# Graph layers with residual norms on one core: row sums on ScalarE, other start addresses of the operands, another order in the beginning

## The chip, the cores and the metric

The program runs on one core of a Trainium2 chip, in one launch. The metric is the device time in microseconds (us). TensorE (PE in the rows) multiplies, and loads its stationary operand by a separate instruction (PEld). VectorE is DVE, ScalarE is ACT, GpSimd is POOL, and SyncE (SP) issues nearly all DMA transfers.

## The reference, cut to what matters

For each of 16 graphs, x is 512x256 and adj is 512x512, all float32:

```python
num_neighbours = adj.sum(axis=-1, keepdims=True)
h = x @ W0 + b0
x1 = layernorm(x + (adj @ h) / num_neighbours)
x2 = relu(adj @ (x1 @ W1) + b1)
x3 = relu(adj @ (x2 @ W2) + b2)
out = layernorm(x1 + adj @ (x3 @ W3) + b3)
```

## The kernel before, in words

**Numbers.** Every matmul operand is split into a high part in the engine's rounded float32 type and a low part, the rest. ScalarE writes the high part (`copy_hi`, line 396), VectorE (`sub_hi`, line 555) or GpSimd (lines 748, 755) the low part. A product is three matmuls, high by high, high by low and low by high (`three_passes`, lines 157 to 159), so a graph takes 228 matmuls.

**Tiles.** There are T = 4 tiles of 128 nodes. A graph goes through eight products. P0 is x W0 (24 matmuls, 256 columns). P1 is adj h (48 matmuls, 258 columns: two columns of ones beside h give the row sums of adj in the same PSUM bank). P2 is the transposed adj x1 (24, 512 columns), P3 the product with W1 (12, 512), P4 with W2 (24, 256), P5 the transposed adj product of s2 (24, 512), P6 with W3 (24, 256), and P7 adj s3 (48, 256). P1 and P7 have adj as the stationary operand and h or s3 as the moving one. In P5, P2, P0, P4 and P6 s2, x1, xT, x2 and x3 are stationary and adj or the weights move. In P3 W1 is stationary and g moves.

**Order.** The order of the instructions of each engine is written out by hand, and semaphores tie the engines together. In the steady state one step (`step`, a loop over three of them) works on three graphs at once: old, new and nxt, in the order P5(old), P2(new), P6(old), P3(new), P7(old), P0(nxt), P4(new), P1(nxt). ScalarE's step follows the same order; between P7 and P1 it takes the four square roots of the second layer norm (`norm2`, line 479), each when VectorE has the moments of a tile, and then the four high parts of h (`h`). P1 waits for all four parts of h. The first two graphs have code of their own ahead of the loop, and the last ones behind it; the three P1, P7 or P5 pieces in them are the same products in smaller pieces.

**Row sums.** After P1, VectorE's `norm1` takes the reciprocal of column 256 of each of the four banks (line 590) and uses it in line 597.

**Start addresses.** On-chip tensors lie behind one another in the order of their declaration, each from the next multiple of 32 bytes. Of every partition's row, by the sizes in the code, these begin at the following remainders modulo 128:

| tensor | before | after |
|---|---|---|
| w, adj | 0 | 0 |
| xT | 0 | 64 |
| s2 | 64 | 0 |
| x1, g, x2, x3, s3 | 64 | 64 |
| h_hi / h_lo, with the bytes from tile to tile | 0 / 32, 1032 | 64 / 64, 1152 |

High and low part have the same remainder but in h before. Slices inside the tensors other than h are whole multiples of 128 bytes apart.

**The beginning.** ScalarE's queue issues the loads of W0 and of the second half of xT, SyncE's all others. A warm-up of 16 matmuls on zeros runs first. P0 of the first graph waits for the whole split of W0. SyncE loads adj of the second graph into the buffer of the first one, and so waits until the first is split (lines 180 to 183).

Of the kernel before, what the change touches and what calls it, by code (L numbers as in the profile page):

```python
# [5 lines left out]
ALU = mybir.AluOpType  # L6
# [4 lines left out]
P = 128  # L11
# [4 lines left out]
WARM = 16  # L16


def build(nc, xT, x, adjT, w0, w1, w2, w3, b0, b1, b2, b3, out):
# [8 lines left out]
    with ExitStack() as ctx:  # L28
# [9 lines left out]
        adj_raw = sb("adj_raw", [P, T, N], F32)  # L38
        w_raw = sb("w_raw", [P, 4, KF, F], F32)
# [28 lines left out]
        inv_rows = sb("inv_rows", [P, T], F32)  # L68
# [4 lines left out]
        std1 = sb("std1", [P, T], F32)  # L73
# [14 lines left out]
        adj_loaded = [sem(f"adj_half{n}_loaded") for n in range(2)]  # L88
        stored = sem("stored")
# [11 lines left out]
        adj0_last_split = sem("adj0_last_split")  # L101
# [58 lines left out]

        block = ctx.enter_context(nc.Block())

        @block.sync
        def _(sp):
# [5 lines left out]
            first_half, second_half = half_of(0, T), half_of(1, T)  # L170
            sp.dma_start(xT_raw[:, first_half], xT[0, :, first_half]).then_inc(xT0_loaded[0], DMA)
            sp.dma_start(adj_raw[:, first_half, :], adjT[0, :, first_half, :]).then_inc(adj_loaded[0], DMA)
            sp.dma_start(adj_raw[:, second_half, :], adjT[0, :, second_half, :]).then_inc(adj_loaded[1], DMA)
# [19 lines left out]
            def load(i):  # L193
# [8 lines left out]
                sp.dma_start(x_raw[:, :, :], x[i]).then_inc(x_loaded, DMA)  # L202

# [14 lines left out]
        def _(pe):  # L218
# [28 lines left out]

            def p1_first(tiles):

                for k in range(T):  # L250
                    pe.wait_ge(h_split, max(k + 1, len(tiles)))
                    if k < T - 1:
                        pe.wait_ge(adj_split, k + 1)
                    else:
                        pe.wait_ge(adj0_last_split, 1)
                    for j in tiles:
                        cols = slice(j * P, (j + 1) * P)
                        mm = three_passes(pe, bank_b[j][:, 0:F + ONES],
                                          (adj_hi[:, 0, k, cols], adj_lo[:, 0, k, cols]),
                                          (h_hi[:, k, :], h_lo[:, k, :]), k == 0, k == T - 1)  # L260
# [14 lines left out]
            def p1(new, tiles=range(T)):  # L275
# [3 lines left out]
                s = slot(new)  # L279
                for j in tiles:  # L280
# [77 lines left out]
            pe.wait_ge(w0_split, 1)  # L358
            p0(FIRST, None, None)
# [34 lines left out]
        def _(act):  # L394
# [81 lines left out]
            def norm2(old, tiles=range(T)):  # L476
                for j in tiles:
                    act.wait_ge(moments2_ready, at(old, T, j + 1))
                    act.activation(std2[:, j:j + 1], moments2[:, j, 1:2], ACT.Sqrt,  # L479
                                   bias=eps_col[:, :]).then_inc(std2_ready, 1)  # L480

            def step(new, last=False, ahead=True):
# [11 lines left out]
                if not last:  # L494
                    norm2(old)
# [27 lines left out]
            norm1(FIRST, None, range(2, T + 1))  # L523
            split_w(1)
            norm1(second, None, range(0, 1))
# [27 lines left out]
        def _(dve):  # L553
# [266 lines left out]
```

## Time and profile before

| | us |
|---|---|
| median of 3 runs | 559.99 (559.52 to 560.68) |
| the profiled execution, time of the run | 559.2 |
| its span, first to last instruction | 557.3 |
| TensorE busy | 545.2, 98% of the span |
| VectorE, ScalarE, GpSimd busy | 352.3, 275.1, 207.3 |

The span leaves 1.9 us of the run's time around it. TensorE's busy time counts overlapping matmuls once, so what a matmul costs is read from the distance of two starts, not from its own duration.

### The profile page before, as it was taken

Reading aid. Unit: us, or ns where it says so; the run is one execution under the profiler, and the core shown is the slowest. Engines: PE = TensorE matmul, PEld = TensorE weight load, DVE = VectorE, ACT = ScalarE, POOL = GpSimd, SP = SyncE. Lnnn points to the kernel's source line nnn. Section 1 sums busy time; section 2 is a strip of 40 time slices with the busy share of each in tenths; the row PEclk is TensorE's granted clock in tenths of the full one; section 3 lists DMA queues with packets and bytes.
Section 4 is the critical chain, followed back from the end, with each engine's and each line's share of the span. In section 5 each row is a group of like instructions: output and inputs, shape, how many; then the busy total and the mean of one; then the engine's idle time right before and its main releaser. Section 6 shows DMA issues by size and latency. Waiting matters only on the chain.

```text
span 557.3 us, 10510 instructions
## 1 busy us (share of the span) xinstructions
PE 545.2 (98%) x3664; PEld 499.7 (90%) x3664; DVE 352.3 (63%) x1075; ACT 275.1 (49%) x645; POOL 207.3 (37%) x224
## 2 busy tenths in 40 slices
PE   8899999999999999999999999999999999999996
PEld 8788989989899898989989899898989989899885
DVE  5764665747567475665747667475665756657455
ACT  5465454463644536454464644636454364543632
POOL 2647226081450906317071350905318072361000
PEclk9999999999999999999999999999999999999999
DMA  6900230503105050140503205040140502200002
GB/s 229 307 13 1 57 135 1 188 2 110 80 0 188 0 180 9 48 140 0 188 0 99 89 0 188 0 169 19 38 151 0 188 1 71 119 1 39 2 1 76
DMA packets 13270, 43.55 MB, mean 78 GB/s; under 512 B 1728, under 2 KB 2496, under 8 KB 13248
## 3 DMA queue, kind: packets, MB, share of 16 engines
q1 hardware_dynamic: 12960, 42.74, 22.4%
q10 hardware_dynamic: 288, 0.52, 0.3%
q8 instruction: 13, 0.21, 0.2%
q14 instruction: 9, 0.07, 0.0%
HBM read 34.87 MB, written 8.39 MB: 78 GB/s over the span
## 4 chain that ended last, share of the span: by engine, by line
PE 94%; issue 2%; DVE 2%; ACT 1%; DMA 1%; POOL 0%; POOLq 0%; DVEq 0%; SPq 0%
PE bank_a L157 16%; PE bank_a L159 16%; PE bank_a L158 16%; PE bank_b L157 15%; PE bank_b L158 15%; PE bank_b L159 15%; DMA adj_raw<-in_adjT 1%; DVE x_lo L555 0%; DVE x L604 0%; DVE v L597 0%; DVE h_lo L555 0%; POOL adj_lo L748 0%; ACT x_hi L459 0%; ACT adj_hi L396 0%; ACT bank_a L461 0%
## 5 line engine op out<-in xcount | busy, mean ns | idle before, releaser
L748 POOL TENSOR_TENSOR adj_lo<-adj_raw,adj_hi 128x512 fp32r<-128x512 f32 x61 | 77.0, 1295 | 288.3 <-ACT adj_hi L396 288.3
L555 DVE TENSOR_TENSOR x_lo<-bank_a,x_hi 128x512 fp32r<-128x512 f32 x64 | 44.3, 692 | 68.7 <-ACT bank_a L461 68.7
L157 PE MATMUL bank_b<-h_hi,adj_hi 128*128 128x258 f32 x256 | 72.4, 283 | 2.2 <-DVE h_lo L555 2.2
L158 PE MATMUL bank_b<-h_lo,adj_hi 128*128 128x258 f32 x256 | 72.3, 282 | 0.0
L159 PE MATMUL bank_b<-h_hi,adj_lo 128*128 128x258 f32 x256 | 72.2, 282 | 0.0
L157 PE MATMUL bank_b<-s_hi,adj_hi 128*128 128x256 f32 x256 | 70.9, 277 | 0.9 <-DVE s_lo L555 0.9
L159 PE MATMUL bank_b<-s_hi,adj_lo 128*128 128x256 f32 x256 | 70.7, 276 | 0.0
L158 PE MATMUL bank_b<-s_lo,adj_hi 128*128 128x256 f32 x256 | 70.7, 276 | 0.0
L436 ACT ACTIVATE std<-moments,eps_col 128x1 f32<-128x1 f32 x64 | 18.9, 295 | 93.3 <-DVE moments L616 93.3
L479 ACT ACTIVATE std<-moments,eps_col 128x1 f32<-128x1 f32 x64 | 18.9, 295 | 80.1 <-DVE moments L656 80.1
L459 ACT ACTIVATE x_hi<-bank_a,b_col 128x512 fp32r<-128x512 f32 x64 | 43.8, 684 | 21.9 <-PE bank_a L159 20.7
L736 POOL TENSOR_TENSOR x1b<-x,b_all 128x256 f32<-128x256 f32 x64 | 46.0, 757 | 18.2 <-DVE x L604 18.2
L555 DVE TENSOR_TENSOR g_lo<-bank_a,g_hi 128x512 fp32r<-128x512 f32 x32 | 22.1, 692 | 47.2 <-ACT g_hi L396 47.2
L157 PE MATMUL bank_a<-adj_hi,x_hi 128*128 128x512 f32 x128 | 50.6, 396 | 0.6 <-DVE x_lo L555 0.6
L157 PEld LDWEIGHTS bank_b<-h_hi,adj_hi 128*128 128x128 f32 x256 | 48.4, 189 | 2.4 <-DVE h_lo L555 2.3
L157 PE MATMUL bank_a<-adj_hi,s_hi 128*128 128x512 f32 x128 | 50.5, 394 | 0.0
L158 PE MATMUL bank_a<-adj_lo,x_hi 128*128 128x512 f32 x128 | 50.5, 394 | 0.0
L159 PE MATMUL bank_a<-adj_hi,x_lo 128*128 128x512 f32 x128 | 50.4, 394 | 0.0
L159 PE MATMUL bank_a<-adj_hi,s_lo 128*128 128x512 f32 x128 | 50.4, 394 | 0.0
L158 PE MATMUL bank_a<-adj_lo,s_hi 128*128 128x512 f32 x128 | 50.4, 394 | 0.0
L157 PEld LDWEIGHTS bank_b<-s_hi,adj_hi 128*128 128x128 f32 x256 | 48.0, 188 | 1.8 <-DVE s_lo L555 1.1
L158 PEld LDWEIGHTS bank_b<-s_lo,adj_hi 128*128 128x128 f32 x256 | 48.0, 188 | 0.7
(84 smaller groups left out, 1586.4 us busy)
## 6 DMA issues: line engine op xcount, KB each, us to landing
adj_raw<-in_adjT SPq DMA_DIRECT2D x32, 512.0 KB, 5.4
x_raw<-in_x SPq DMA_DIRECT2D x16, 512.0 KB, 7.4
xT_raw<-in_xT SPq DMA_DIRECT2D x15, 512.0 KB, 6.6
out_y<-y SPq DMA_DIRECT2D x15, 512.0 KB, 2.9
w_raw<-in_w SPq DMA_DIRECT2D x3, 256.0 KB, 4.3
out_y<-y SPq DMA_DIRECT2D x4, 128.0 KB, 1.9
w_raw<-in_w ACTq DMA_DIRECT2D x1, 256.0 KB, 3.5
xT_raw<-in_xT SPq DMA_DIRECT2D x1, 256.0 KB, 3.7
```

The lines of the kernel that those rows point to most:

```text
L157: pe.matmul(acc, st[0], mv[0], start=start, stop=False)
L158: pe.matmul(acc, st[0], mv[1], start=False, stop=False)
L159: return pe.matmul(acc, st[1], mv[0], start=False, stop=stop)
L436: act.activation(std1[:, j:j + 1], moments1[:, j, 1:2], ACT.Sqrt, bias=eps_col[:, :]).then_inc(std1_ready, 1)
L459: act.activation(hi[:, f, :], bank_a[f][:, :], ACT.Relu, bias=bias[:, f:f + 1])
L479: act.activation(std2[:, j:j + 1], moments2[:, j, 1:2], ACT.Sqrt, bias=eps_col[:, :]).then_inc(std2_ready, 1)
L555: return dve.tensor_tensor(lo, full, hi.bitcast(F32), ALU.subtract)
L736: pool.tensor_tensor(x1b[:, slot(batch), j, :], x1[:, j, :], b3_all[:, :], ALU.add).then_inc(x1b_ready, 1)
L748: pool.tensor_tensor(adj_lo[:, s, k, :], adj_raw[:, k, :], adj_hi[:, s, k, :].bitcast(F32), ALU.subtract).then_inc(done, 1)
```

## The change

ScalarE sums the rows of adj: SyncE loads adj, untransposed, into a new buffer (1 MB for each graph from the third on), and a copy with an accumulated output on ScalarE gives the sum of a tile's rows, one behind each square root of `norm2`. From the third graph on P1 has 256 columns, and VectorE takes one reciprocal of all four sums. The first two graphs keep the ones. The tensors are declared in another order, with the remainders of the table above, and h's tiles are 288 elements apart. In the beginning SyncE issues W0 and both halves of xT first, P0 starts on the high parts alone, h comes ahead of the adj splits, and the second graph's adj goes into the new buffer without the wait. Two more warm-up matmuls run.

```diff
-WARM = 16
+H_ROW = 288
+WARM = 18
...
         w_hi, w_lo = pair("w", [P, 4, KF, F])
+        adj_hi, adj_lo = pair("adj", [P, RING, T, N])
+        s2_hi, s2_lo = pair("s2", [P, T, F])
+        inv_rows = sb("inv_rows", [P, T], F32)
+        std1 = sb("std1", [P, T], F32)
+        x1_hi, x1_lo = pair("x1", [P, T, F])
         xT_hi, xT_lo = pair("xT", [P, T, KF, P])
-        adj_hi, adj_lo = pair("adj", [P, RING, T, N])
-        h_hi, h_lo = pair("h", [P, T, F + ONES])
-        x1_hi, x1_lo = pair("x1", [P, T, F])
         g_hi, g_lo = pair("g", [P, KF, N])
         x2_hi, x2_lo = pair("x2", [P, KF, N])
-        s2_hi, s2_lo = pair("s2", [P, T, F])
         x3_hi, x3_lo = pair("x3", [P, KF, N])
         s3_hi, s3_lo = pair("s3", [P, T, F])
+        h_hi, h_lo = pair("h", [P, T, H_ROW])
...
             sp.wait_ge(xT_split, 2)
             sp.dma_start(xT_raw[:, :], xT[1]).then_inc(xT_loaded, DMA)
-            sp.wait_ge(adj_split, T)
-            sp.wait_ge(adj0_last_split, 1)
-            sp.dma_start(adj_raw[:, first_half, :], adjT[1, :, first_half, :]).then_inc(adj_loaded[0], DMA)
-            sp.dma_start(adj_raw[:, second_half, :], adjT[1, :, second_half, :]).then_inc(adj_loaded[1], DMA)
+            for half, tiles in enumerate(halves):
+                sp.dma_start(adj1_raw[:, tiles, :], adjT[1, :, tiles, :]).then_inc(adj1_loaded[half], DMA)
...
                 sp.wait_ge(xb_ready, i * T)
                 sp.dma_start(x_raw[:, :, :], x[i]).then_inc(x_loaded, DMA)
+                sp.wait_ge(rows_ready, i * T)
+                sp.dma_start(adj_rows[:, :, :], adj[i]).then_inc(rows_loaded, DMA)
...
+            def p0_first():
+                for j in range(T):
+                    half = j // (T // 2)
+                    pe.wait_ge(xT_hi_ready, half + 1)
+                    for k in range(KF):
+                        pe.matmul(bank_b[j][:, 0:F], xT_hi[:, j, k, :], w_hi[:, 0, k, :], start=k == 0, stop=False)
+                    pe.wait_ge(w0_split, 1)
+                    for k in range(KF):
+                        pe.matmul(bank_b[j][:, 0:F], xT_hi[:, j, k, :], w_lo[:, 0, k, :], start=False, stop=False)
+                    pe.wait_ge(xT_split, half + 1)
+                    for k in range(KF):
+                        mm = pe.matmul(bank_b[j][:, 0:F], xT_lo[:, j, k, :], w_hi[:, 0, k, :],
+                                       start=False, stop=k == KF - 1)
+                    mm.then_inc(p0_done, 1)
...
+                width = F + ONES if new is second else F
...
+            def row_sum(nxt, j):
+                if j == 0:
+                    act.wait_ge(rows_loaded, at(nxt, DMA, -DMA))
+                act.activation(adj_rows[:, j, :], adj_rows[:, j, :], ACT.Copy,
+                               accum_out=rows[:, j:j + 1]).then_inc(rows_ready, 1)
...
                     act.activation(std2[:, j:j + 1], moments2[:, j, 1:2], ACT.Sqrt,
                                    bias=eps_col[:, :]).then_inc(std2_ready, 1)
+                    if nxt is not None:
+                        row_sum(nxt, j)
...
+                    if a == 0 and not from_columns:
+                        dve.wait_ge(rows_ready, at(new, T, T))
+                        dve.reciprocal(inv_rows[:, :], rows[:, :]).then_inc(inv_rows_ready, 1)
```

How the instructions move on ScalarE, in the step between the last Relu ahead of P7 and the high parts of h; before:

```order
L461 ACTIVATE bank_a<-bank_a,b_col 128x512
L479 ACTIVATE std<-moments,eps_col 128x1 x4
L421 REGISTER_ALU
L396 ACTIVATE h_hi<-bank_b 128x256
L421 REGISTER_ALU
L396 ACTIVATE h_hi<-bank_b 128x256
```

and after, at the same place:

```order
L502 ACTIVATE bank_a<-bank_a,b_col 128x512
L521 ACTIVATE std<-moments,eps_col 128x1
L456 REGISTER_ALU
L457 ACTIVATE adj_rows,rows<-adj_rows 128x512
L521 ACTIVATE std<-moments,eps_col 128x1
L457 ACTIVATE adj_rows,rows<-adj_rows 128x512
L521 ACTIVATE std<-moments,eps_col 128x1
L457 ACTIVATE adj_rows,rows<-adj_rows 128x512
L521 ACTIVATE std<-moments,eps_col 128x1
L457 ACTIVATE adj_rows,rows<-adj_rows 128x512
L462 REGISTER_ALU
L424 ACTIVATE h_hi<-bank_b 128x256
```

Four copies of 512 columns now stand between the square roots and ahead of h's high parts.

SyncE's queue from the program's start; before:

```order
L171 DMA xT_raw<-in_xT 128x512
L172 DMA adj_raw<-in_adjT 128x1024
L173 DMA adj_raw<-in_adjT 128x1024
L174 DMA x_raw<-in_x 128x1024
L175 DMA b_all<-in_b 128x256
L178 DMA xT_raw<-in_xT 128x1024
L182 DMA adj_raw<-in_adjT 128x1024
L183 DMA adj_raw<-in_adjT 128x1024
```

and after:

```order
L184 DMA w_raw<-in_w 128x512
L186 DMA xT_raw<-in_xT 128x512 x2
L188 DMA adj_raw<-in_adjT 128x1024 x2
L189 DMA x_raw<-in_x 128x1024
L190 DMA b_all<-in_b 128x256
L193 DMA xT_raw<-in_xT 128x1024
L195 DMA adj_rows<-in_adjT 128x1024 x2
```

W0 and the second half of xT came from ScalarE's queue before; now one queue has all, and the second graph's adj follows the second xT without a wait between them.

## Rows read from the trace of the kernel before

**Rows 1.** The page, busy time of each engine

```profile
PE 545.2 (98%) x3664; PEld 499.7 (90%) x3664; DVE 352.3 (63%) x1075; ACT 275.1 (49%) x645; POOL 207.3 (37%) x224
```

**Rows 2.** The page, the chain that ended last, by engine

```profile
PE 94%; issue 2%; DVE 2%; ACT 1%; DMA 1%; POOL 0%; POOLq 0%; DVEq 0%; SPq 0%
```

**Rows 3.** Timeline of TensorE, each product's first matmul; start, duration in us

```profile
175.53 0.40 PE L157 MATMUL bank_a<-adj_hi,s_hi 128*128 128x512 f32 x1
...
181.14 0.39 PE L157 MATMUL bank_a<-adj_hi,x_hi 128*128 128x512 f32 x1
...
186.74 0.28 PE L157 MATMUL bank_b<-w_hi,x_hi 128*128 128x256 f32 x1
...
189.47 0.39 PE L157 MATMUL bank_a<-g_hi,w_hi 128*128 128x512 f32 x1
...
192.22 0.28 PE L157 MATMUL bank_b<-s_hi,adj_hi 128*128 128x256 f32 x1
...
197.66 0.28 PE L157 MATMUL bank_b<-w_hi,xT_hi 128*128 128x256 f32 x1
...
200.53 0.28 PE L157 MATMUL bank_a<-w_hi,x_hi 128*128 128x256 f32 x1
...
203.36 0.28 PE L157 MATMUL bank_b<-h_hi,adj_hi 128*128 128x258 f32 x1
...
209.12 0.40 PE L157 MATMUL bank_a<-adj_hi,s_hi 128*128 128x512 f32 x1
```

**Rows 4.** The same of the last graphs: P7's first half, P4, P7's third tile, P5

```profile
528.08 0.28 PE L157 MATMUL bank_b<-s_hi,adj_hi 128*128 128x256 f32 x1
...
530.80 0.28 PE L157 MATMUL bank_a<-w_hi,x_hi 128*128 128x256 f32 x1
...
533.63 0.28 PE L157 MATMUL bank_b<-s_hi,adj_hi 128*128 128x256 f32 x1
...
535.05 0.39 PE L157 MATMUL bank_a<-adj_hi,s_hi 128*128 128x512 f32 x1
```

**Rows 5.** The same of the beginning, up to the first step's P5

```profile
1.20 3.78 PE L246 MATMUL bank_a<-zeros 128*128 128x256 f32 x16 [1.20 <-DVE zeros L673]
6.21 0.55 PE L157 MATMUL bank_b<-w_hi,xT_hi 128*128 128x256 f32 x1 [1.24 <-DVE xT_lo L555]
...
10.99 0.28 PE L157 MATMUL bank_b<-h_hi,adj_hi 128*128 128x258 f32 x1
...
16.73 0.28 PE L157 MATMUL bank_a<-w_hi,xT_hi 128*128 128x256 f32 x1
...
21.91 0.36 PE L157 MATMUL bank_b<-h_hi,adj_hi 128*128 128x258 f32 x1 [2.15 <-DVE h_lo L555]
...
41.19 0.40 PE L157 MATMUL bank_a<-adj_hi,s_hi 128*128 128x512 f32 x1
```

**Rows 6.** Timeline of the other engines in the beginning

```profile
4.31 0.43 DVE L681 CAST w_hi<-w_raw 128x512 fp32r<-128x512 f32 x1 [3.02 <-DMA w_raw<-in_w]
4.55 0.63 ACT L396 ACTIVATE xT_hi<-xT_raw 128x512 fp32r<-128x512 f32 x1 [1.39 <-DMA xT_raw<-in_xT]
...
15.95 1.15 ACT L396 ACTIVATE adj_hi<-adj_raw 128x512 fp32r<-128x512 f32 x2 [3.33 <-DMA adj_raw<-in_adjT]
...
19.32 2.49 POOL L748 TENSOR_TENSOR adj_lo<-adj_raw,adj_hi 128x512 fp32r<-128x512 f32 x2
...
19.76 1.42 DVE L555 TENSOR_TENSOR h_lo<-bank_a,h_hi 128x256 fp32r<-128x256 f32 x4 [0.94 <-ACT h_hi L396]
```

**Rows 7.** Groups by form; busy us, mean ns | idle before

```profile
L396 ACT ACTIVATE adj_hi<-adj_raw 128x512 fp32r<-128x512 f32 x64 | 39.1, 617 | 3.6 <-DMA adj_raw<-in_adjT 3.6
```

**Rows 8.** Timeline of ScalarE and VectorE, from norm2's first square root to h

```profile
195.49 0.29 ACT L479 ACTIVATE std<-moments,eps_col 128x1 f32<-128x1 f32 x1 [1.84 <-DVE moments L656]
...
199.46 0.64 ACT L396 ACTIVATE h_hi<-bank_b 128x256 fp32r<-128x256 f32 x2
...
200.12 1.46 DVE L555 TENSOR_TENSOR h_lo<-bank_b,h_hi 128x256 fp32r<-128x256 f32 x4
```

More of the change, by code:

```diff
@@ L67, in build @@
         y = sb("y", [P, T, F], F32)
-        inv_rows = sb("inv_rows", [P, T], F32)
+        rows = sb("rows", [P, T], F32)
         stats1 = sb("stats1", [P, T, 6], F32)
@@ L88, in build @@
         adj_loaded = [sem(f"adj_half{n}_loaded") for n in range(2)]
+        adj1_loaded = [sem(f"adj1_half{n}_loaded") for n in range(2)]
+        rows_loaded = sem("rows_loaded")
+        rows_ready = sem("rows_ready")
+        inv_rows_ready = sem("inv_rows_ready")
         stored = sem("stored")
@@ L168, in half_of @@
                 return slice(half * n // 2, (half + 1) * n // 2)
[L170 to L173, printed above, removed]
+            sp.sem_inc(rows_ready, 2 * T)
+            halves = [half_of(half, T) for half in range(2)]
+            sp.dma_start(w_raw[:, 0, :, :], w0).then_inc(w_loaded[0], DMA)
+            for half, tiles in enumerate(halves):
+                sp.dma_start(xT_raw[:, tiles], xT[0, :, tiles]).then_inc(xT0_loaded[half], DMA)
+            for half, tiles in enumerate(halves):
+                sp.dma_start(adj_raw[:, tiles, :], adjT[0, :, tiles, :]).then_inc(adj_loaded[half], DMA)
             sp.dma_start(x_raw[:, :, :], x[0]).then_inc(x_loaded, DMA)
@@ L178, in _ @@
             sp.dma_start(xT_raw[:, :], xT[1]).then_inc(xT_loaded, DMA)
-            sp.wait_ge(adj_split, T)
-            sp.wait_ge(adj0_last_split, 1)
-            sp.dma_start(adj_raw[:, first_half, :], adjT[1, :, first_half, :]).then_inc(adj_loaded[0], DMA)
-            sp.dma_start(adj_raw[:, second_half, :], adjT[1, :, second_half, :]).then_inc(adj_loaded[1], DMA)
+            for half, tiles in enumerate(halves):
+                sp.dma_start(adj1_raw[:, tiles, :], adjT[1, :, tiles, :]).then_inc(adj1_loaded[half], DMA)
             sp.dma_start(w_raw[:, 1, :, :], w1).then_inc(w_loaded[1], DMA)
@@ L474, in x3, with norm2 @@
                 relu_split(p5_done, old, f, b2_col, x3_hi, x3_hi_ready)
-            def norm2(old, tiles=range(T)):
+            def norm2(old, tiles=range(T), nxt=None):
                 for j in tiles:
@@ L507, in _ @@
             split_xT(FIRST, 1)
+            h(FIRST, tiles=range(0, 2))
             split_adj(FIRST, 0)
             split_adj(FIRST, 1)
-            h(FIRST, tiles=range(0, 2))
+            h(FIRST, tiles=range(2, T))
             split_adj(FIRST, 2)
             split_adj(FIRST, 3)
-            h(FIRST, tiles=range(2, T))
             split_xT(second, 0)
@@ L522, in _ @@
             h(second, bank_a)
[L523 removed]
+            norm1(FIRST, None, range(2, 3))
             split_w(1)
+            norm1(FIRST, None, range(3, T + 1))
             norm1(second, None, range(0, 1))
@@ L685, in _ @@
             split_xT(FIRST, 1)
+            h(FIRST, tiles=range(0, 2))
             split_adj(FIRST, 0)
-            h(FIRST, tiles=range(0, 1))
             split_adj(FIRST, 1)
-            h(FIRST, tiles=range(1, 2))
+            h(FIRST, tiles=range(2, T))
             split_adj(FIRST, 2)
-            h(FIRST, tiles=range(2, T))
+            split_adj(FIRST, 3)
             split_xT(second, 0)
@@ L742, in split_w, with split_adj @@
                                    ALU.subtract).then_inc(w_split, 1)
-            def split_adj(nxt, done, tiles=range(T)):
+            def split_adj(nxt):
                 s = slot(nxt)
-                for k in tiles:
+                raw = adj1_raw if nxt is second else adj_raw
+                for k in range(T):
                     pool.wait_ge(adj_hi_ready, at(nxt, T, k + 1))
-                    pool.tensor_tensor(adj_lo[:, s, k, :], adj_raw[:, k, :], adj_hi[:, s, k, :].bitcast(F32),
-                                       ALU.subtract).then_inc(done, 1)
+                    pool.tensor_tensor(adj_lo[:, s, k, :], raw[:, k, :], adj_hi[:, s, k, :].bitcast(F32),
+                                       ALU.subtract).then_inc(adj_split, 1)
             def split_xT(nxt):
@@ L771, in _ @@
             pool.wait_ge(adj_split, T)
-            split_adj(second, adj_split)
+            split_adj(second)
             add_b0(second)
@@ L803 @@
         "adjT": adj.reshape(NB, P, T, P, T).transpose(0, 3, 4, 2, 1).reshape(NB, P, T, N),
+        "adj": adj.reshape(NB, P, T, N),
     }
```

53 lines of the change are left out of this document (28 added, 25 removed).

## The prediction, as put on record before the changed kernel ran

> **What bounds the kernel now.** First the page: TensorE is busy 545.2 of 557.3 us [rows 1], and the chain that ended last is 94% TensorE [rows 2]. A faster ScalarE or VectorE is worth nothing by itself; what counts is how far apart TensorE's matmuls start, and where it waits. So I read its timeline. One step is 33.59 us [rows 3], the distance of two P5, and no start in that list has an idle time in front of it. The distances of the nine starts, divided by the matmuls in between, give what one matmul costs in each product:
>
> - P5 5.61 us / 24 = 234 ns, P2 5.60 / 24 = 233 ns, P3 2.75 / 12 = 229 ns, all with 512 columns.
> - P6 2.73 / 24 = 114 ns, P7 5.44 / 48 = 113 ns, P4 2.83 / 24 = 118 ns, P0 2.87 / 24 = 120 ns, with 256 columns, and P1 5.76 / 48 = 120 ns with 258.
>
> The same columns cost 113 ns in one product and 120 in another. Set beside the table of start addresses, the dear one of the 256-column products is P0, the only one whose stationary and moving operand both begin at remainder 0; P6, P7 and P4 have 64 on one side and 0 on the other. P1 mixes many remainders, since its tiles are 1032 bytes apart. The two extra columns of P1 explain 2/256 of 113 ns, 0.9 ns, and not 6.7.
>
> P4 shows a second thing: it has P6's remainders and costs 4.5 ns more. The end of the program helps. There P7's first half starts at 528.08 and takes 2.72 us / 24 = 113 ns, P4 directly behind it 2.83 / 24 = 118 ns, and P7's third tile behind that 1.42 / 12 = 118 ns, though it is the same product as the one at 113 [rows 4]. So a pace once taken is handed on by unbroken matmuls of 256 columns, and the passage from P7 (moving operand at 64) to a product with its stationary operand at 64 costs the fast pace.
>
> **The beginning** is 41.19 us to the first P5 [rows 5]. P0 starts at 6.21, after 1.24 us of waiting for a low part of xT, and its 24 matmuls take 4.78 us, against 2.87 later. TensorE also waits 2.15 us ahead of 21.91.
>
> The terms are taken against the profiled execution: span 557.3 us, time 559.2, which is 0.8 us below the median of the runs, 559.99. I carry the differences over to the median.
>
> **The change, part by part.**
>
> *P1, width and start of h.* 14 graphs (the third to the last) run with 256 columns and h at 64 against adj at 0, which is what P7 has. Bounds: 113 ns, P7's pace [rows 3], and 120, no gain. P1 follows P4, and P4 follows P0. In the tail the same passage, P4 to P7's third tile, stays at 118 [rows 4], so I take 117.9: 14 x 48 x 2.1 ns = 1.4 us. Lower bound 0, upper 14 x 48 x 6.7 ns = 4.5 us.
>
> *P0, xT at 64.* It now has P4's and P6's remainders. It follows P7, exactly the passage that gives 118 in the tail. 14 x 24 x (119.6 - 117.9) ns = 0.6 us; upper bound with P6's 113.8, 2.0 us. P4 behind it stays at 117.9; with the fast pace it would give 14 x 24 x 4.1 ns = 1.4 us.
>
> *P5, s2 at 0.* Now both operands begin at 0, at 512 columns. No row shows that pair at this width. The nearest rows: with 64 stationary and 0 moving 233.3 ns, with 0 and 64 229 (P3), so the start addresses do matter at 512 too. The step between paces at 256 columns is 6.7 ns (113.3 to 120.0). [...] I bound the effect at 6.7 ns per matmul to either side and take the gain, 16 x 24 x 6.7 ns = 2.6 us, as P3 shows that 233 is not the floor. This is the weakest term. P2 keeps its remainders and its 233 ns.
>
> [...]
>
> *Row sums.* Four ScalarE copies of 512 columns per step with an accumulated output. No row has that form. Bounds: 0.62 us, the plain copy [rows 7], and that plus a square root's 0.29 [rows 8], 0.91. I take 0.75. What hides them: the first square root starts at 195.49, h's first high part at 199.46, the last low part ends at 200.12 + 1.46 = 201.58, and P1 starts at 203.36. With a row sum of R behind each of the four square roots (0.2 us each), four high parts (1.4 us together) and one low part behind them (0.45), h is complete at 195.49 + 0.8 + 4R + 1.85 = 198.14 + 4R. That reaches 203.3 at R = 1.29, so at 0.91 nothing is late. Queued behind them on ScalarE are h and then s2, for which P1 and the next P5 wait; P5 is 5.8 us later. VectorE loses four reciprocals of one column and gains one of four columns, beside TensorE. The new load, 1 MB per graph, is issued a step ahead of its use, behind the other three. Its wait in SyncE's queue is for row sums that ScalarE has done by then, ahead of h. All cost 0.
>
> *The beginning.* W0 (256 KB) is now alone at the head of the queue. Before, W0 and half of xT came together at 4.31 and 4.55 [rows 6]; at the same rate W0 is there some 0.8 us earlier and xT no later. TensorE then needs only the high parts: 4.55 + 0.63 = 5.2, when 18 warm-up matmuls of 0.21 us end as well (1.20 + 3.84 = 5.04). P0 starts 1.1 us earlier, at 5.1. I carry 1.1 through P1 and to the second graph's P0: 15.6 in place of 16.73. That ends 24 x 0.118 = 2.8 us later, 18.5; the last high and low part of its h are 0.8 us more, 19.2. GpSimd's splits of the second adj ended at 19.32 + 2.49 = 21.81, because their transfer waited and ScalarE stood 3.33 us for it [rows 6]. With that transfer earlier by more than 2 us they end near 19. So the second graph's P1 starts at 19.2 in place of 21.91. Of this 2.7 us not all is kept: VectorE's last low part of h ended at 19.76 + 1.42 = 21.18 and now at 19.2, and the layer norm of the first graph hangs on VectorE behind it. I take 2.0 us, between 1.1 (the earlier P0 alone) and 3.0.
>
> *Sum.* 2.0 + 1.4 + 0.6 + 2.6 = 6.6 us. 559.99 - 6.6 = **553.4 us** (profiled 552.6).
>
> **The rivals.**
>
> 1. *The fast pace everywhere.* If P0 takes P6's 113.8 ns and hands it on, P0, P4 and P1 give 2.0 + 1.4 + 4.5 = 7.9 us in place of 2.0: 547.5. For it: P7 and P6 run at it for whole products. Against: the passage in the tail. Chance 0.18.
> 2. *P5 gains nothing.* 559.99 - 4.0 = 556.0. P5 and P2 are at 233 whatever stood ahead of them. Chance 0.17.
> 3. *Remainders don't matter at all.* The 120 ns of P0 come from what surrounds it. Then only the beginning and 14 x 48 x 0.9 ns = 0.6 us are left: 557.4. P0 against P6 speaks against it. Chance 0.07.
> 4. *Both at 0 is dear at 512 as it is at 256.* P5 loses 2.6 us: 558.6. P0 speaks for it, as the only product in the trace with that pair. Chance 0.10.
> 5. *Slower: the row sums delay h.* Place: ScalarE between P7 and P1. From R = 1.29 us on, P1 starts 4 x (R - 1.29) late in each of 14 steps; at R = 1.41 that eats the whole gain, and at 1.5 it costs 11.8 us: 565.2. The bound of 0.91 speaks against it, the lack of any row with an accumulated output for it. Chance 0.06.
>
> **How the numbers follow.** The forecast has 0.42, and the rivals the rest. From 546.5 to 558.0 the range holds the forecast and rivals 1 to 3, 0.84, less something for their own errors. A difference under 0.2%, 1.1 us, can't be told from none here. Forecast and rivals 1 to 4 are all faster by more, of rival 4 a part is not; rival 5 is slower in most of its width: faster 0.91, same 0.04, slower 0.05.
>
> **What would show it.** In the timeline of the changed kernel the step falls from 33.59 to about 33.28 us: P5 near 227 ns per matmul, P2 at 233, P0, P4 and P1 near 118, P6 and P7 unchanged. At 113 in P0 rival 1 holds, at 233 or 240 in P5 rivals 2 or 4. The row sums' group should show 0.62 to 0.91 us and no wait of P1 for h_lo in a step. The first P5 of the loop should start near 39.2. The forecast is wrong if P1 waits in the steps, or if TensorE's pace in P2, P3, P6 or P7 moves, which no term has.

## The result, and the profile after

The changed kernel takes 557.86 us (median of 16 runs, 556.26 to 559.76) against 559.88 us before (16 runs beside it): a ratio of 0.9967, 95% interval 0.9956 to 0.9979. The direction was forecast; the size, 6.6 us, was not: 2.0 us came. The profiled execution took 557.75 us, its span is 555.8.

The page's busy times and chain by engine, which answer to [rows 1, 2]:

```profile
PE 543.4 (98%) x3666; PEld 499.7 (90%) x3666; DVE 350.8 (63%) x1034; ACT 307.4 (55%) x757; POOL 207.9 (37%) x223
...
PE 93%; DVE 3%; DMA 2%; ACT 1%; issue 0%; SPq 0%; DVEq 0%
```

ScalarE has 32 us more to do, and TensorE bounds the kernel as before. DMA now has 2% of the chain. TensorE's timeline, the first matmul of each product in one step, as [rows 3]:

```profile
176.18 0.39 PE L166 MATMUL bank_a<-adj_hi,s_hi 128*128 128x512 f32 x1
...
181.63 0.40 PE L166 MATMUL bank_a<-adj_hi,x_hi 128*128 128x512 f32 x1
...
187.23 0.28 PE L166 MATMUL bank_b<-w_hi,x_hi 128*128 128x256 f32 x1
...
190.06 0.40 PE L166 MATMUL bank_a<-g_hi,w_hi 128*128 128x512 f32 x1
...
192.86 0.28 PE L166 MATMUL bank_b<-s_hi,adj_hi 128*128 128x256 f32 x1
...
198.51 0.28 PE L166 MATMUL bank_b<-w_hi,xT_hi 128*128 128x256 f32 x1
...
201.24 0.28 PE L166 MATMUL bank_a<-w_hi,x_hi 128*128 128x256 f32 x1
...
203.96 0.28 PE L166 MATMUL bank_b<-h_hi,adj_hi 128*128 128x256 f32 x1
...
209.56 0.39 PE L166 MATMUL bank_a<-adj_hi,s_hi 128*128 128x512 f32 x1
```

The distance of two P5 is 33.38 us in place of 33.59. Divided by the matmuls in between, these starts and those of the other profiles give this table: ns per matmul and us per step, each over the 14 steps, which agree within 1 to 2 ns per matmul. "First P5" is that of the loop. In f1 and g2 the 0.12 us of each zero matmul are in the step and in no product.

| kernel | P5 | P2 | P6 | P3 | P7 | P0 | P4 | P1 | step us | first P5 us |
|---|---|---|---|---|---|---|---|---|---|---|
| before | 233.4 | 233.3 | 113.8 | 229.0 | 113.3 | 119.8 | 117.9 | 120.0 | 33.587 | 41.19 |
| changed | 227.2 | 233.3 | 117.8 | 233.5 | 117.8 | 113.8 | 113.3 | 116.6 | 33.387 | 42.62 |
| e1, x1 at 0 | 227.3 | 226.6 | 117.8 | 233.5 | 117.8 | 113.8 | 113.3 | 116.6 | 33.227 | 43.07 |
| e2, before, s2 at 0 | 226.6 | 233.3 | 117.8 | 233.5 | 117.8 | 120.0 | 117.9 | 120.0 | 33.793 | 41.73 |
| e3, no row sums | 228.6 | 233.3 | 117.8 | 233.6 | 117.8 | 113.8 | 113.3 | 120.1 | 33.587 | 42.06 |
| e5, s2 at 64 | 232.9 | 233.3 | 117.8 | 233.5 | 117.8 | 113.8 | 113.3 | 116.7 | 33.527 | 43.45 |
| f1, zero matmul | 226.7 | 226.6 | 114.0 | 229.0 | 113.3 | 117.8 | 117.9 | 117.8 | 33.233 | 41.30 |
| f2, h rows 1280 | 227.7 | 226.6 | 117.8 | 233.6 | 117.8 | 113.8 | 113.3 | 113.4 | 33.080 | 42.61 |
| g2, two zero matmuls | 227.7 | 226.6 | 114.0 | 229.0 | 113.4 | 114.0 | 113.3 | 113.4 | 32.967 | 41.05 |
| g3, g at 0 | 227.7 | 226.6 | 117.8 | 229.0 | 117.8 | 113.8 | 113.3 | 113.4 | 33.027 | 40.25 |

The step gained 0.15 us in P5, 0.14 in P0, 0.11 in P4 and 0.16 in P1, and lost 0.10 in P6, 0.05 in P3 and 0.21 in P7. That is -0.20 us, 14 times: -2.8 us. The beginning lost 1.4, the end gained 0.1: 1.5 us less in all, as the spans say.

The beginning after; TensorE first, as [rows 5], then the others:

```profile
10.54 0.36 PE L166 MATMUL bank_b<-h_hi,adj_hi 128*128 128x258 f32 x1 [1.41 <-DVE adj_lo L596]
...
17.21 0.28 PE L166 MATMUL bank_a<-w_hi,xT_hi 128*128 128x256 f32 x1
...
22.39 0.39 PE L166 MATMUL bank_b<-h_hi,adj_hi 128*128 128x258 f32 x1 [2.28 <-DVE h_lo L596]
...
42.62 0.40 PE L166 MATMUL bank_a<-adj_hi,s_hi 128*128 128x512 f32 x1
```

```profile
6.52 0.63 ACT L424 ACTIVATE xT_hi<-xT_raw 128x512 fp32r<-128x512 f32 x1 [1.64 <-DMA xT_raw<-in_xT]
...
9.04 1.15 ACT L424 ACTIVATE adj_hi<-adj_raw 128x512 fp32r<-128x512 f32 x2 [1.34 <-DMA adj_raw<-in_adjT]
...
13.92 1.15 ACT L424 ACTIVATE xT_hi<-xT_raw 128x512 fp32r<-128x512 f32 x2 [2.16 <-DMA xT_raw<-in_xT]
15.44 1.15 ACT L424 ACTIVATE adj_hi<-adj_rows 128x512 fp32r<-128x512 f32 x2 [0.36 <-DMA adj_rows<-in_adjT]
...
16.22 5.51 POOL L797 TENSOR_TENSOR adj_lo<-adj_rows,adj_hi 128x512 fp32r<-128x512 f32 x4 [0.33 <-ACT adj_hi L424]
...
20.92 1.42 DVE L596 TENSOR_TENSOR h_lo<-bank_a,h_hi 128x256 fp32r<-128x256 f32 x4 [0.94 <-ACT h_hi L424]
```

P0 starts at 5.20, 0.1 us behind the forecast, and P1 at 10.54 after a wait of 1.41 us for adj's low part, since adj landed at 9.0; before, ScalarE had it at 7.25. The second graph's xT is on the chain: issued at 7.90, landed at 13.92 (6.0 us). On VectorE, the reciprocals of the row sums and the layer norm of the first graph stand behind its split, so h's low parts begin at 20.92, 1.16 us later than before, and end at 22.34. The second adj, though it no longer waits, was there for ScalarE at 15.44 in place of 15.95, and GpSimd's low parts of it ended at 21.73 in place of 21.80. So the second graph's P1 starts at 22.39, 0.5 us later than before, not 2.7 earlier. Then the clock fell. Windows of TensorE after and before; the third figure from the right is the granted clock:

```profile
20.00:22.40 2.40, 0.12 (x2) 0.01 (x1) 1.48 (x6) 1.69 (x6) 2.40 (x4) 1.00 0.90 306
22.40:24.80 2.40, 2.40 (x13) 2.40 (x14) 2.04 (x10) 0.47 (x2) 1.52 (x3) 0.68 0.71 217
24.80:27.00 2.20, 2.20 (x7) 1.67 (x6) 1.84 (x7) 1.10 (x4) 1.70 (x2) 0.57 0.74 296
```

```profile
19.60:21.90 2.30, 0.15 (x2) 0.02 (x1) 2.10 (x8) 0.94 (x4) 2.30 (x3) 1.00 0.92 249
21.90:24.30 2.40, 2.39 (x15) 2.10 (x16) 2.09 (x7) 0.60 (x2) 2.23 (x3) 1.00 0.77 271
```

In both TensorE stood nearly idle for over 2 us. Before, the granted clock stayed at 1.00. After, it was 0.50 from 23.4 to 26.4 us; the pieces of P1 and P2 behind the wait took 2.08 + 7.09 us against 1.68 + 6.53, 0.96 us more. That is not what the clock cost. The runs g1 and g2 below have one beginning and one code up to the first P5 of the loop; the clock fell in the profile of g2 alone:

```profile
20.89 0.39 PE L163 MATMUL bank_b<-h_hi,adj_hi 128*128 128x258 f32 x1 [1.21 <-DVE h_lo L595]
...
23.00:24.00 1.00, 1.00 (x5) 0.80 (x5) 0.85 (x4) 0.95 (x3) 0.20 (x1) 1.00 0.70 221
24.00:25.00 1.00, 0.44 (x3) 0.03 (x1) 1.00 (x4) 0.00 (x0) 1.00 (x2) 1.00 0.92 360
```

```profile
20.88 0.39 PE L163 MATMUL bank_b<-h_hi,adj_hi 128*128 128x258 f32 x1 [2.27 <-DVE h_lo L600]
...
23.00:24.00 1.00, 1.00 (x3) 0.81 (x4) 0.85 (x4) 0.94 (x3) 0.21 (x1) 0.50 0.85 270
24.00:25.00 1.00, 1.00 (x3) 0.76 (x3) 1.00 (x4) 0.00 (x0) 1.00 (x2) 0.50 0.82 332
```

P1 starts at 20.89 and 20.88, and the first P5 of the loop at 41.06 and 41.05. At a granted clock of 1.00 (g1) TensorE is done sooner with each piece and waits 1.25 us for VectorE's low parts of x1; at 0.50 (g2) it works through that time. So in this beginning VectorE's layer norm of the first graph sets the pace up to P2's end, and the fall costs nothing up to P5. The changed kernel and f2 are such a pair too: P1 at 22.39 and 22.42, first P5 at 42.62 and 42.61, and f2's granted clock stayed at 1.00 from 18 to 34 us.

The row sums (group rows by form) cost ScalarE 616 ns for the copy and 186 for a second instruction that reads the accumulator; the last one occupies it from 200.24 to h at 200.85:

```profile
L457 ACT ACTIVATE adj_rows<-adj_rows 128x512 f32<-128x512 f32 x56 | 34.5, 616 | 0.0
...
L457 ACT ACTIVATION_READ_ACCUMULATOR adj_rows<-adj_rows 128x1 f32 x56 | 10.4, 186 | 0.0
```

```profile
200.24 0.61 ACT L457 ACTIVATE adj_rows<-adj_rows 128x512 f32<-128x512 f32 x1
200.76 0.19 ACT L457 ACTIVATION_READ_ACCUMULATOR adj_rows<-adj_rows 128x1 f32 x1
200.85 1.18 ACT L424 ACTIVATE h_hi<-bank_b 128x256 fp32r<-128x256 f32 x4
```

### The profile page after: what moved, and what is told of

The parts are those of the page before. It is cut to its first block, busy times and chain, and to the rows that moved or that the text cites. A ratio compares the mean times of both kernels' runs of the same rounds, so it can differ in the third digit from the quotient of the medians.

```text
span 555.8 us, 10623 instructions
## 1 busy us (share of the span) xinstructions
PE 543.4 (98%) x3666; PEld 499.7 (90%) x3666; DVE 350.8 (63%) x1034; ACT 307.4 (55%) x757; POOL 207.9 (37%) x223
## 4 chain that ended last, share of the span: by engine, by line
PE 93%; DVE 3%; DMA 2%; ACT 1%; issue 0%; SPq 0%; DVEq 0%
PE bank_a L166 16%; PE bank_a L167 16%; PE bank_a L168 16%; PE bank_b L166 15%; PE bank_b L167 15%; PE bank_b L168 15%; DMA xT_raw<-in_xT 2%; DVE xT_lo L596 0%; DVE x_lo L596 0%; DVE v L645 0%; DVE x L652 0%; DVE stats L656 0%; DVE h_lo L596 0%; ACT x_hi L500 0%; ACT xT_hi L424 0%
## 5 line engine op out<-in xcount | busy, mean ns | idle before, releaser
L797 POOL TENSOR_TENSOR adj_lo<-adj_raw,adj_hi 128x512 fp32r<-128x512 f32 x56 | 70.8, 1298 | 274.8 <-ACT adj_hi L424 274.8
L166 PE MATMUL bank_b<-h_hi,adj_hi 128*128 128x256 f32 (+1 forms) x256 | 72.1, 282 | 4.0 <-DVE h_lo L596 2.3
L167 PE MATMUL bank_b<-h_lo,adj_hi 128*128 128x256 f32 (+1 forms) x256 | 71.9, 281 | 0.0
L168 PE MATMUL bank_b<-h_hi,adj_lo 128*128 128x256 f32 (+1 forms) x256 | 71.6, 280 | 0.0
L778 POOL TENSOR_TENSOR xb<-x_raw,b_all 128x256 f32<-128x256 f32 x64 | 47.2, 774 | 12.8 <-DMA b_all<-in_b 11.5
```

The lines of the kernel that those rows point to most:

```text
L166: pe.matmul(acc, st[0], mv[0], start=start, stop=False)
L167: pe.matmul(acc, st[0], mv[1], start=False, stop=False)
L168: return pe.matmul(acc, st[1], mv[0], start=False, stop=stop)
L778: pool.tensor_tensor(xb[:, j, :], x_raw[:, j, :], b0_all[:, :], ALU.add).then_inc(xb_ready, 1)
L797: pool.tensor_tensor(adj_lo[:, s, k, :], raw[:, k, :], adj_hi[:, s, k, :].bitcast(F32), ALU.subtract).then_inc(adj_split, 1)
```

## The experiments

They ran in three sets, each beside runs of its own of the kernel before, as the changed kernel did (559.88 us): e1 to e4 (median 559.62 us), e5, f1, f2 and b1 (559.60), and g1 to g3 and b2 (559.42). Across sets a few tenths of a us, the drift of these medians, can't be told from none. The ratios are to that kernel. Differences in the steps come from the profiles and are far sharper: the changed kernel, e4, b1 and b2 each take 467.42 us for the 14 steps. The beginning is not: with the same loads in the same queue and order, the first P5 stands between 41.30 and 43.45 in the six profiles of the changed kernel, e1, e3, e5, f1 and f2, and the second graph's xT lands between 12.48 and 14.58.

**e1: x1 at 0 too**

```diff
         s2_hi, s2_lo = pair("s2", [P, T, F])
+        x1_hi, x1_lo = pair("x1", [P, T, F])
         inv_rows = sb("inv_rows", [P, T], F32)
         std1 = sb("std1", [P, T], F32)
-        x1_hi, x1_lo = pair("x1", [P, T, F])
```

> The changed kernel with x1_hi and x1_lo at remainder 0 as well, all else as in it. Theory A (a pace is taken at the passage between two products and handed on by unbroken matmuls; the start addresses of the product itself set only which paces there are): P2 falls from 233 to about 227 ns per matmul, and as P5 and P2 now have the same remainders, what P2 hands to P6 may change too: P6, P3 and P7, which cost 118, 233 and 118 ns in the changed kernel, either stay or go back to 114, 229 and 113; if they go back, P0 and P4 should turn from 114 and 113 to 118. Step 33.1 to 33.3 us. Theory B (each product's cost hangs on its own start addresses and on nothing ahead of it): only P2 moves, by -6 ns, and the step falls from 33.387 to 33.24 us.

555.87 us (6 runs; ratio to before 0.9939, 0.9928 to 0.9951). Only P2 moved, from 233.3 to 226.6 ns, 0.16 us a step. This is what x1 at 64 costs the changed kernel, 2.2 us over 14 steps. The paces of P6, P3 and P7 stayed; it does not decide between the theories, as A allowed both.

**e2: the kernel before, s2 alone at 0**

```diff
+        s2_hi, s2_lo = pair("s2", [P, T, F])
         h_hi, h_lo = pair("h", [P, T, F + ONES])
...
-        s2_hi, s2_lo = pair("s2", [P, T, F])
```

> The kernel before with the s2 pair declared ahead of h, so at remainder 0; every other remainder as before, no row sums, old beginning. Theory A: P5 227 ns, P2 233, and then P6 118, P3 233 and P7 118 as in the changed kernel, from this one move alone; the step gets 0.15 us from P5 and loses 0.37 in P6, P3 and P7, so about 33.8 us, slower than before by 3 us in all, unless P0 and P4 gain from P7's other pace (up to 0.2 us a step). Theory B (P6, P3 and P7 got dearer by something else of the change, as the row sums on ScalarE or the other place of h): P5 227 and all others as before, step 33.44 us, 2.3 us faster in all.

562.44 us (one run; before 559.62), step 33.793. P5 gained its 6.8 ns, and P6, P3 and P7, which don't touch s2, took the slow pace, exactly that of the changed kernel:

```profile
187.94 0.28 PE L157 MATMUL bank_b<-w_hi,x_hi 128*128 128x256 f32 x1
...
190.76 0.40 PE L157 MATMUL bank_a<-g_hi,w_hi 128*128 128x512 f32 x1
...
193.57 0.28 PE L157 MATMUL bank_b<-s_hi,adj_hi 128*128 128x256 f32 x1
...
199.22 0.29 PE L157 MATMUL bank_b<-w_hi,xT_hi 128*128 128x256 f32 x1
```

P6 takes 2.82 us, P3 2.81 and P7 5.65. Theory B of e1, that a product's cost is its own addresses, is refuted. The move also shifts h, x1, g and x2 by 8192 bytes with their remainders kept, but the operands of P6 and P7 (x3, s3, w and adj) did not move at all, and both changed. It is one run; the paces are the same in all 14 steps.

**e3: no row sums**

```diff
-                width = F + ONES if new is second else F
+                width = F + ONES
...
-                    norm2(old, nxt=nxt)
+                    norm2(old)
...
-                from_columns = new is FIRST or new is second
+                from_columns = True
```

> The changed kernel without the row sums: no load of adj in rows, no copies with an accumulated output, the ones columns and the four reciprocals in every graph, P1 with 258 columns throughout. Theory A: P6, P3 and P7 stay at 118, 233 and 118 ns, P0 at 114; P1 goes from 116.6 to about 120, the step from 33.387 to about 33.55 us, total some 2 us above the changed kernel. Theory B (ScalarE's copies or the added load slow TensorE's products beside them): P7 returns to 113 ns, as the copies run beside it, and the step falls below 33.3 us.

560.00 us (12 runs, 558.88 to 562.29; 1.0016, 1.0003 to 1.0029), step 33.587: the new addresses by themselves won nothing, the step is that of before. The row sums and P1's 256 columns are the 0.20 us a step, 0.17 of it in P1. P7 keeps 117.8 ns with the copies beside it and without them, so they don't slow it.

**e4: the old beginning**, that is the kernel before with the row sums and the new addresses; the cut is against the changed kernel

```diff
-WARM = 18
+WARM = 16
...
-            for half, tiles in enumerate(halves):
-                sp.dma_start(adj1_raw[:, tiles, :], adjT[1, :, tiles, :]).then_inc(adj1_loaded[half], DMA)
+            sp.wait_ge(adj_split, T)
+            sp.wait_ge(adj0_last_split, 1)
+            sp.dma_start(adj_raw[:, first_half, :], adjT[1, :, first_half, :]).then_inc(adj_loaded[0], DMA)
+            sp.dma_start(adj_raw[:, second_half, :], adjT[1, :, second_half, :]).then_inc(adj_loaded[1], DMA)
...
-            pe.wait_ge(w0_hi_ready, 1)
-            p0_first()
+            pe.wait_ge(w0_split, 1)
+            p0(FIRST, None, None)
...
+            act.dma_start(w_raw[:, 0, :, :], w0).then_inc(w_loaded[0], DMA)
+            half = slice(T // 2, T)
+            act.dma_start(xT_raw[:, half], xT[0, :, half]).then_inc(xT0_loaded[1], DMA)
```

> The kernel before with the row sums and the new start addresses, but with its own beginning (order of loads, P0 behind the whole split of W0, adj of the second graph behind the first one's split, 16 warm-up matmuls). If the new beginning is what lost 1.4 us up to the first P5 of the loop (42.62 against 41.19 us in the profiles): first P5 near 41.2 us, steps 33.39 us, about 556.4 us, 1.5 us below the changed kernel, and with its runs closer together. If the loss comes from the new addresses in the beginning's products: first P5 near 42.6 us and the time of the changed kernel, 557.9.

556.70 us (5 runs, 556.31 to 557.17; 0.9945, 0.9933 to 0.9958), 1.2 us below the changed kernel, 0.9 when each is taken against the kernel before beside it; the two intervals just touch. So the new beginning does not gain the 2.0 us that I had forecast, and most likely loses about 1. Both expectations missed the profile: the first P5 is at 42.15, between the 41.2 and the 42.6. The second adj reached ScalarE at 16.51 in place of 15.95, GpSimd's low parts ended at 22.36, and P1 started at 22.46 in place of 21.91. Behind that the granted clock was 0.51 from 23 to 26 us, where before's profile has 1.00; there 0.4 us more were lost, by the clock or not. So of the 1.4 us between the profiles of before and the changed kernel 1.0 is in e4 too, and only the runs can tell the beginnings apart.

**e5: s2 back at 64**

```diff
+        inv_rows = sb("inv_rows", [P, T], F32)
+        std1 = sb("std1", [P, T], F32)
         s2_hi, s2_lo = pair("s2", [P, T, F])
-        inv_rows = sb("inv_rows", [P, T], F32)
-        std1 = sb("std1", [P, T], F32)
```

> The changed kernel with s2 back at remainder 64 (and x1 at 64), so P5 and P2 as in the kernel before, while xT and h stay at 64. Theory A (a pace is taken at a passage and handed on; P0's 114 ns in the changed kernel came from P7 being slow ahead of it): P5 and P2 233, P6, P3 and P7 back at 114, 229 and 113, and P0 and P4 at 118, as P4 behind the fast P7 at the end of the kernel before; P1 118 to 120. Step about 33.45 us. Theory B (P0 and P4 are fast by their own addresses): P0 and P4 at 114 and 113, P1 116.6, P6, P3, P7 fast as well, step about 33.2 us.

560.72 us (one run), step 33.527. Both expectations missed: P5 lost its gain, and P6, P3 and P7 stayed slow. So s2 at 0 is enough to bring the slow pace (e2), and not needed for it once the other edits are in. P0 and P4 are fast, behind a slow P7.

**f1: e1 with a zero matmul ahead of P6**

```diff
+                def ready(j):
+                    pe.wait_ge(reader, at(read, T, j + 1))
+                    if j == 0:
+                        pe.matmul(bank_b[0][:, 0:F], zeros[:, 0:P], zeros[:, :], start=True, stop=True)
```

> The kernel of e1 (s2 and x1 at 0) with one matmul of zeros by zeros, 256 columns, both operands at remainder 64, put ahead of P6's first in each step; it writes a bank that P6 then starts anew. It costs about 113 ns a step. Theory A: the passage into P6 is another one, so its pace can flip from 117.8 to 113.8 ns, and P3 and P7 with it (229 and 113.3; together -0.37 us), and then P0 and P4 flip the other way, from 114 and 113 to 118 (+0.21). Step 33.15 to 33.25 us. Theory B: all paces stay, the step is e1's 33.227 + 0.11 = 33.34 us.

554.19 us (one run). With one matmul put in and no address changed, everything behind it flipped as theory A said:

```profile
185.13 0.28 PE L358 MATMUL bank_b<-zeros 128*128 128x256 f32 x1
185.25 0.28 PE L163 MATMUL bank_b<-w_hi,x_hi 128*128 128x256 f32 x1
...
187.99 0.39 PE L163 MATMUL bank_a<-g_hi,w_hi 128*128 128x512 f32 x1
...
190.74 0.28 PE L163 MATMUL bank_b<-s_hi,adj_hi 128*128 128x256 f32 x1
...
196.18 0.28 PE L163 MATMUL bank_b<-w_hi,xT_hi 128*128 128x256 f32 x1
...
199.00 0.28 PE L163 MATMUL bank_a<-w_hi,x_hi 128*128 128x256 f32 x1
...
201.83 0.28 PE L163 MATMUL bank_b<-h_hi,adj_hi 128*128 128x256 f32 x1
```

P6 2.74 us, P3 2.75 and P7 5.44 are back at the pace of before, and P0 (2.82) and P4 (2.83) went from fast to slow. The sum is level with e1 in the steps, 33.233 against 33.227; the 1.7 us between the two times are in the beginning (first P5 at 41.30 against 43.07), whose code is the same.

**f2: e1 with h's tiles 1280 bytes apart**

```diff
-H_ROW = 288
+H_ROW = 320
```

> The kernel of e1 with h's tiles 1280 bytes apart in place of 1152, so that they keep one remainder modulo 256 (64), as s3's tiles, which are 1024 bytes apart. P1 costs 116.6 ns with a pattern of 12 matmuls that repeats. If only the remainder modulo 128 counts: P1 stays at 116.6 and the step at 33.227 us. If the remainder modulo 256 counts too: P1 takes P7's form with h's pace handed on from P4, 113.3 ns, and the step falls by 48 x 3.3 ns to 33.07 us.

553.27 us (one run). P1 fell from 116.6 to 113.4 ns and the step by 0.147 us. The remainder modulo 128 is not the whole of it: 1152 and 1280 bytes have the same.

**b1: two queues in the beginning**

```diff
-            sp.dma_start(w_raw[:, 0, :, :], w0).then_inc(w_loaded[0], DMA)
-            for half, tiles in enumerate(halves):
-                sp.dma_start(xT_raw[:, tiles], xT[0, :, tiles]).then_inc(xT0_loaded[half], DMA)
+            sp.dma_start(xT_raw[:, halves[0]], xT[0, :, halves[0]]).then_inc(xT0_loaded[0], DMA)
...
+            act.dma_start(w_raw[:, 0, :, :], w0).then_inc(w_loaded[0], DMA)
+            half = slice(T // 2, T)
+            act.dma_start(xT_raw[:, half], xT[0, :, half]).then_inc(xT0_loaded[1], DMA)
```

> The changed kernel with W0 and the second half of the first xT issued from ScalarE's queue as in the kernel before, and SyncE's queue beginning with the first half of xT; nothing else is changed. In the changed kernel's profile the second half of xT landed 4.70 us after its issue and the second graph's xT 6.00 us after its own, at 13.92 against 11.47 or earlier before. Theory Q (one queue is slow to bring many transfers of 256 KB one after another): xT's second half lands by 5.8, the second graph's xT by 12, the second graph's P1 starts 1 to 2 us earlier (near 21), and the time falls by 1 us or more to about 556.8. Theory O (the loss comes from the order of work on VectorE and ScalarE and from the earlier load of the second adj, which shares the transfer engines): no change, 557.9.

556.24 us (6 runs, 555.27 to 556.77; 0.9926, 0.9900 to 0.9951), 1.6 us below the changed kernel, 1.3 by the medians of before beside each. The intervals don't touch, though one run of before at 563.74 pulls b1's ratio down and widens its interval.

```profile
12.12 1.15 ACT L422 ACTIVATE xT_hi<-xT_raw 128x512 fp32r<-128x512 f32 x2 [1.23 <-DMA xT_raw<-in_xT]
```

The second graph's xT is there at 12.1 in place of 13.9, and its P1 starts at 21.24 in place of 22.39. The first xT's second half came no earlier (6.82 against 6.52), so of theory Q the later transfers hold and the first does not. All five profiles with two queues have the second xT by 12.12; of the six with one queue, five have it at 13.46 or later and f1 at 12.48. The edit also takes W0 from ahead of xT in SyncE's queue; the number of queues and the order in them are not separated.

**b2: b1, the second adj waits as before**

```diff
+            sp.wait_ge(adj_split, T)
             for half, tiles in enumerate(halves):
                 sp.dma_start(adj1_raw[:, tiles, :], adjT[1, :, tiles, :]).then_inc(adj1_loaded[half], DMA)
```

> The kernel of b1 (changed kernel, two queues in the beginning) with the wait of before put back: the loads of the second graph's adj stand behind the split of the first one's, though they go into their own buffer. In b1 they were issued at 8.57, landed by 14.2 and GpSimd had split them at 20.6, 0.6 us ahead of the second graph's P1 at 21.24. If the early load is what b1 has ahead of the old beginning (556.24 against 556.7 us): ScalarE's split moves to about 16, GpSimd's end to 22 and P1 to 22, 0.5 to 1 us later, 556.8 us. If VectorE's chain alone sets that P1: no change, 556.2 us.

557.19 us (5 runs, 557.03 to 557.72; 0.9962, 0.9949 to 0.9976), 0.95 us above b1, with no run of either inside the other's range. The second graph's P1 starts at 21.95, behind GpSimd's last low part of adj at 21.86, as expected. The early load is worth about that 0.95. The rest of the new beginning, b2 against e4, would be 0.5 us dearer than the old one; their intervals overlap, so that is not shown.

**g1: x1 at 0, h's tiles 1280 bytes apart, two queues**

```diff
-H_ROW = 288
+H_ROW = 320
...
+        x1_hi, x1_lo = pair("x1", [P, T, F])
         inv_rows = sb("inv_rows", [P, T], F32)
...
+            act.dma_start(w_raw[:, 0, :, :], w0).then_inc(w_loaded[0], DMA)
```

> All edits that the runs so far favour: the changed kernel with x1 at 0 too, h's tiles 1280 bytes apart, and W0 and the second half of the first xT from ScalarE's queue. If the parts add up: steps of 33.08 us as in f2, first P5 of the loop near 41.5 as in b1, so 14 x (33.587 - 33.080) = 7.1 us less than before and 0.3 us in the tail: 552.0 to 552.6 us. If the old layout's beginning or the clock takes some back: up to 554.

551.34 us (4 runs; 0.9853, 0.9838 to 0.9868). The parts add up, with 0.7 us more than the 552.0 expected at best; step 33.080, first P5 at 41.06.

**g2: g1 with zero matmuls ahead of P6 and P0**

```diff
+                        if j == 0:
+                            pe.matmul(bank_b[0][:, 0:F], zeros[:, 0:P], zeros[:, :], start=True, stop=True)
```

> The kernel of g1 with a zero matmul ahead of P6 and another ahead of P0 in each step. Theory A (the pace is taken at a passage, and a further passage flips it): P6, P3 and P7 fast (114, 229, 113) from the first, and P0, P4 and P1 fast (114, 113, 113) from the second, which undoes the flip to 118 that f1 showed behind a fast P7. It costs 2 x 0.115 us and wins 0.37 against g1: step near 32.94 us, 2 us less than g1. If the second one does not flip: P0, P4 and P1 at 118, step near 33.4 us, 4 us more than g1.

549.40 us (5 runs; 0.9821, 0.9808 to 0.9835), the fastest of all. The second one flips P0 back (2.73 us for P0, 2.72 for P4, 5.45 for P1), so all 256-column products run at 113 to 114 ns:

```profile
194.86 0.28 PE L249 MATMUL bank_b<-zeros 128*128 128x256 f32 x1
194.98 0.28 PE L163 MATMUL bank_b<-w_hi,xT_hi 128*128 128x256 f32 x1
...
197.71 0.28 PE L163 MATMUL bank_a<-w_hi,x_hi 128*128 128x256 f32 x1
...
200.43 0.28 PE L163 MATMUL bank_b<-h_hi,adj_hi 128*128 128x256 f32 x1
...
205.88 0.39 PE L163 MATMUL bank_a<-adj_hi,s_hi 128*128 128x512 f32 x1
```

**g3: g1 with g at 0**

```diff
+        g_hi, g_lo = pair("g", [P, KF, N])
         inv_rows = sb("inv_rows", [P, T], F32)
```

> The kernel of g1 with the g pair at remainder 0 as well, so that all three products of 512 columns (P5, P2, P3) have both operands at 0. Theory A: P3 goes from 233.5 to 227 ns (-0.08 us a step), and the passages into P3 and P7 are others, so P7 (118) may become fast (-0.22 us) and P0 and P4 slow (+0.21), or not: step 32.9 to 33.2 us. If a product's pace hung only on its own addresses: P3 -0.08 us, step 33.00 us, all else the same.

550.19 us (5 runs; 0.9840, 0.9827 to 0.9854). P3 fell to 229.0, not to 227, and P7 behind it stayed slow, though before 229.0 in P3 went with a fast P7. The step, 33.027, fits both expectations, so g3 decides nothing. Its first P5 is at 40.25, 0.8 us before g1's, with the same code for the beginning; it is no more than the beginning varies.

## Why the prediction was wrong, by its own steps

In the profiles 1.5 us came where 6.6 were forecast. The beginning is 3.4 short (-1.4 for 2.0), and the steps with P5's other two 1.7 (2.8 and about 0.1 for 4.6). In each of the two a step of the reasoning failed; the points below name it:

- *P5, s2 at 0: right.* 6.2 ns per matmul for 6.7 forecast, 2.1 us in the 14 steps. The weakest term held, and e2 shows it alone.
- *P1: size off.* 3.4 ns in place of 2.1; it followed a fast P4, and its own tile distance kept it from 113.4 (f2).
- *P0: size off.* 6.0 ns in place of 1.7, and P4 gained 4.6 for nothing forecast. I took the passage from P7 to P0 as one that costs the fast pace. With xT at 64 it swaps the pace: behind a fast P7 P0 runs at 117.8 (f1), behind a slow one at 113.8 (changed kernel, e5).
- *"P6 and P7 unchanged", and P3: the step that failed.* They lost 0.36 us a step, 5.1 us in 14. P0, P4 and P1 together gained 5.8 where 2.0 was forecast, which hides most of it: that the steps came out only 1.5 us short is in part luck. I had read that a pace is handed on [rows 4], and applied it to P0, P4 and P1 alone. Behind a product whose addresses move, the others can change as well, so also behind P5 (e2). Rival 1 (fast everywhere) and the forecast both left that out. g2 is the fast pace of rival 1, and it needed two extra matmuls; in the changed kernel P0 and P4 took that pace because P7 had lost it.
- *Row sums: right.* 0.61 us each on ScalarE for 0.75 forecast, hidden; P1 waits in no step. Without them the kernel is 2.1 us slower by the medians and 2.8 by the steps (e3).
- *The beginning: wrong in sign, the larger loss.* P0 did start 1.0 us earlier. I assumed that no transfer lands later, and that only VectorE's old chain follows. All loads through one queue brought adj 1.8 us and the second xT 2.4 us or more later, and VectorE's layer norm of the first graph stood behind that xT. I had the second graph's h complete at 19.2 and GpSimd's low parts of adj near 19; they ended at 22.34 and 21.73. Even with h in time, P1 could not have started 2.7 us earlier, since the second adj gained 0.5 us by leaving out its wait and not the "more than 2" that I took. In the runs the old beginning is about 1 us faster (e4) where I had it 2.0 us slower. b1 gives back 1.3 to 1.6, so the way the loads are queued is what lost it.
- *Rival 3, that remainders don't matter: refuted.* With x1 at 64 or at 0, and every other matmul operand at its remainder, P2 takes 233.3 or 226.6 ns per matmul (the changed kernel and e1), and likewise with s2 P5 takes 233.4 or 226.6 (before and e2). By what mechanism, no run shows.

Open: by what mechanism a pace is taken and handed on, and which of xT, h and P1's 256 columns brought the slow one in e5. Theory A gave its direction right in e2 and f1, and missed e5. The wide spread of the changed kernel's runs (3.5 us) is not the clock: ten of the 16 have the same mean granted clock, 0.997, and lie between 556.26 and 559.76, and the one at 1.000 took 557.11. As the beginning varies by 2.2 us between profiles and the 14 steps don't, it most likely comes from when the first loads land; the record has no landings for the other runs.

## What to carry to other kernels

Where TensorE is the bound, divide start distances by product and set the start addresses of both operands beside them; 64 bytes decided 3 to 5% (P2 226.6 ns in e1 against 233.3 in the changed kernel, P0 113.8 in the changed kernel against 120.0 in e2). Change one address at a time and read the products behind the changed one too, since a pace is handed on: in e2 s2 alone changed its remainder, and P6, which doesn't read it, went from 113.8 to 117.8 ns. In a beginning, follow each load to its landing, try the loads on two queues (b1 was 1.3 to 1.6 us faster), and compare several executions: one profile of it says little below 1 us, as the first P5 stood between 41.30 and 43.45 in six. Where the granted clock falls, look for what TensorE would otherwise have waited for before the fall is given a price: with 1.00 (g1) and 0.50 (g2) the first P5 stood at 41.06 and 41.05 us.

## What the runs showed of the hardware that I had not expected

- Unbroken matmuls of 256 columns with 64 on one side and 0 on the other keep one of two paces, 113.3 or 117.8 ns, over up to 96 matmuls, and a single matmul of zeros flips it for the next 84, 12 of them of 512 columns (f1).
- With both operands at 0, 512 columns cost 226.6 ns against 233.3 with 64 and 0; at 256 columns both at 0 is the dear pair, 120.0 against 113.3 to 117.9.
- Tiles 1152 and 1280 bytes apart, with equal remainders modulo 128, cost 116.6 and 113.4 ns.
- An accumulated output adds an instruction of 186 ns.
- A granted clock of 0.5 for over 2 us cost nothing up to the first P5 where VectorE's chain sets the pace: 41.05 us (g2) against 41.06 (g1).
